# A convolution stage in which ScalarE makes a third tap for half of each piece, and VectorE takes 18 steps instead of 20

## The reference

```python
x = x + _L0_conv_ref(_gn(x), L0_conv_finsler_params)
x = x + _L1_conv_ref(_gn(x), L1_conv_proj_w, ...)
```

```python
out = jnp.einsum('oi,bihw->bohw', proj_w[:, :, 0, 0], x) + proj_b[None, :, None, None]
h = jax.lax.conv_general_dilated(out, dw_w, window_strides=(1, 1), padding=((1, 1), (1, 1)),
                                 feature_group_count=C, dimension_numbers=('NCHW', 'OIHW', 'NCHW'))
h = h + dw_b[None, :, None, None]
```

## Time and profile before

| | |
|---|---|
| median of 3 runs | 10253.23 us |
| the profiled execution: its time, its span | 10254.56 us, 10252.8 us |
| busy share of the span | VectorE 97%, ScalarE 90%, GpSimd 87%, TensorE 84% |
| convolution stage, from the first copy out of PSUM to the last sum | 8700.5 to 9487.6 us |
| resampling stage | 9487.6 us to the end |

### The profile page before, as it was taken

The page is one execution under the profiler, slowest core; times in us unless marked ns, Lnnn a source line. Parts: engine busy times, 40 slices in busy tenths (PEclk is TensorE's granted clock), DMA queues, the critical chain, the costliest instruction groups (busy, mean ns, idle before and its releaser), DMA issues. The chain is left out here.

```text
span 10252.8 us, 72623 instructions
## 1 busy us (share of the span) xinstructions
PE 8565.8 (84%) x18068; PEld 3322.9 (32%) x18068; DVE 9963.9 (97%) x5623; ACT 9179.9 (90%) x6861; POOL 8875.6 (87%) x3274
## 2 busy tenths in 40 slices
PE   2888888888888888888888888888888887998899
PEld 0333333333333333333333333333333333443333
DVE  8999999999999999999999999999999999999999
ACT  2999999999999999999999999999999997888776
POOL 2889888898988999898988888898889887777998
PEclk9999999999999999999999999999999999999999
DMA  8788878888888888888888888888888876444776
GB/s 322 149 157 151 155 155 159 158 160 158 159 157 159 159 158 159 153 159 156 160 155 156 159 158 160 159 158 157 160 159 158 158 141 137 178 182 187 268 282 258
DMA packets 442070, 1751.43 MB, mean 171 GB/s; under 512 B 23888, under 2 KB 130384, under 8 KB 392784
## 3 DMA queue, kind: packets, MB, share of 16 engines
q0 software_dynamic: 278528, 1110.51, 60.9%
q1 hardware_dynamic: 163152, 636.41, 16.6%
HBM read 391.58 MB, written 201.33 MB: 58 GB/s over the span
## 5 line engine op out<-in xcount | busy, mean ns | idle before, releaser
L589 PE MATMUL chain<-dx,mats 128*128 128x512 f32 x10240 | 4979.5, 632 | 940.6 <-ACT chain L639 940.3
L530 POOL TENSOR_TENSOR m<-m,u 128x2048 f32<-128x2048 f32 x1024 | 4338.1, 4350 | 187.1 <-ACT m L621 185.9
L589 PEld LDWEIGHTS chain<-dx,mats 128*128 128x128 f32 x10240 | 1917.0, 197 | 4002.9 <-ACT chain L639 2095.8
L718 DVE SCALAR_TENSOR_TENSOR acc_a<-m,kt,acc_a 128x2048 f32<-128x2048 f32 x1344 | 3162.5, 2353 | 38.2 <-issue 2.4
L639 ACT ACTIVATE chain<-chain,gap_r 128x1024 f32<-128x1024 f32 x2560 | 2694.2, 1086 | 232.2 <-PE chain L589 230.5
L718 DVE SCALAR_TENSOR_TENSOR acc_a<-t,kt,acc_a 128x2048 f32<-128x2048 f32 x1024 | 2411.9, 2355 | 34.2
L501 POOL DMA_DIRECT2D t<-u x1024 | 1486.4, 1563 | 652.8 <-ACT t L621 635.1
L526 POOL TENSOR_TENSOR m<-u,m 128x2048 f32<-128x2048 f32 x384 | 1707.1, 4445 | 0.0
L621 ACT ACTIVATE t<-dx,gap_l 128x2048 f32<-128x2048 f32 x768 | 1540.5, 2006 | 0.4 <-issue 0.4
L589 PE MATMUL chain<-u,mats 128*128 128x512 f32 x3072 | 1456.0, 605 | 71.8 <-ACT chain L639 71.8
L718 DVE SCALAR_TENSOR_TENSOR acc_a<-u,kt,acc_a 128x2048 f32<-128x2048 f32 x576 | 1357.0, 2356 | 20.5
(11 more groups left out here) (149 smaller groups left out, 6876.4 us busy)
## 6 DMA issues: line engine op xcount, KB each, us to landing
t<-u POOLq DMA_DIRECT2D x1024, 1059.0 KB, 8.7
u<-x_dram SPq DMA_DIRECT2D x32, 2688.0 KB, 30.6
xt<-x_dram SPq DMA_DIRECT2D x32, 2048.0 KB, 14.2
x_scratch<-x SPq DMA_DIRECT2D x64, 1024.0 KB, 10.7
h_scratch<-h SPq DMA_DIRECT2D x32, 2048.0 KB, 7.2
both<-h_scratch SPq DMA_DIRECT2D x64, 1024.0 KB, 9.3
out_dram<-res SPq DMA_DIRECT2D x64, 1024.0 KB, 4.9
both<-x_scratch SPq DMA_DIRECT2D x28, 2304.0 KB, 12.6
```

The source lines that it names most:

```text
L530: nc.gpsimd.tensor_tensor(m_tile(j), m_tile(j), rows, ALU.add).then_inc(m_ready, 1)
L589: added = nc.tensor.matmul(chain[h][:, r:r + 2, :], weight, src[:, top:top + 2, dj:dj + W], start=False, stop=True, skip_group_check=True)
L718: nc.vector.scalar_tensor_tensor(out=acc_a[:], in0=src, scalar=k_base, in1=acc_a[:], op0=ALU.subtract, op1=ALU.max).then_inc(a_done, 1)
```

## The change

The second half of each window (its rows 8 to 15; parts q = 2 and 3) gets one tap more from ScalarE: tap 6, which VectorE took before. It goes into the upper half of `tap_b`, once GpSimd has added what lay there, and GpSimd has a fifth add for it. VectorE's chains for q = 2 and 3 have four steps instead of five, 18 in a window. The counts on which the engines wait are changed accordingly. Besides, `tap_a` starts 2 elements (8 bytes) further on in its buffer.

```diff
-        tap_a = [sb(f"tap_a{s}", [P, WR, W]) for s in range(2)]
+        tap_a = [sb(f"tap_a{s}", [P, WR * W + 4])[:, 2:WR * W + 2].rearrange("p (r w) -> p r w", w=W)
+                 for s in range(2)]
...
-        ADDS = 2 * HALVES
-
-        at_step = sorted(((part, k) for part in range(NWIN * PARTS) for k in range(CHAIN)),
-                         key=lambda x: x[0] * CHAIN + 2 * x[1])
+        ACTS = (TAPS_ACT, TAPS_ACT + 1)
+        ALL_ACTS, ADDS = sum(ACTS), sum(ACTS)
+
+        def chain_of(q):
+            return CHAIN + TAPS_ACT - ACTS[q * HALVES // PARTS]
+
+        WSTEPS = sum(chain_of(q) for q in range(PARTS))
+        at_step = sorted(((n * PARTS + q, k) for n in range(NWIN) for q in range(PARTS) for k in range(chain_of(q))),
+                         key=lambda x: x[0] // PARTS * WSTEPS + x[0] % PARTS * CHAIN + 2 * x[1])
...
                 def tap(n, half, which):
                     act.wait_ge(evacuated, n * NPROJ + (4, NPROJ)[half])
+                    lo = half * HALF_ROWS
                     if which == 0:
                         if n >= 2:
-                            act.wait_ge(pool_adds, (n - 2) * ADDS + (2 * half + 2))
+                            act.wait_ge(pool_adds, (n - 2) * ADDS + (2, ADDS)[half])
                             act.wait_ge(h_summed, (n - 2) * 2 + 2)
-                        dst = tap_a[n % 2]
+                        dst = tap_a[n % 2][:, lo:lo + HALF_ROWS, :]
+                    elif which == 1:
+                        if n >= 1:
+                            act.wait_ge(pool_adds, (n - 1) * ADDS + (4, 3)[half])
+                        dst = tap_b[:, lo:lo + HALF_ROWS, :]
                     else:
-                        if n >= 1:
-                            act.wait_ge(pool_adds, (n - 1) * ADDS + (2 * half + 1))
-                        dst = tap_b
-                    t = 9 - TAPS_ACT + which
+                        act.wait_ge(pool_adds, n * ADDS + 1)
+                        dst = tap_b[:, 0:HALF_ROWS, :]
+                    t = 9 - TAPS_ACT + which if which < TAPS_ACT else 9 - TAPS_ACT - 1
...
                     tap(n, 1, 0)
                     tap(n, 1, 1)
+                    tap(n, 1, 2)
...
-                        pool.wait_ge(h_chain, steps_done[n * PARTS + 2 * half + 1, CHAIN - 1])
+                        if half == 1:
+
+                            pool.wait_ge(act_taps, n * ALL_ACTS + ALL_ACTS)
+                            nc.gpsimd.tensor_tensor(tap_a[n % 2][:, rows, :], tap_a[n % 2][:, rows, :],
+                                                    tap_b[:, 0:HALF_ROWS, :], ALU.add).then_inc(pool_adds, 1)
+                            pool.wait_ge(pool_adds, n * ADDS + 4)
+
+                        pool.wait_ge(h_chain, part_done(n * PARTS + 2 * half + 1))
...
-                    if k == CHAIN - 1:
+                    if k == chain_of(q) - 1:
```

More of the change, by code:

```diff
@@ L830, in convolution, with part_done @@
         HALF_ROWS = WR // HALVES
-        ADDS = 2 * HALVES
-        at_step = sorted(((part, k) for part in range(NWIN * PARTS) for k in range(CHAIN)),
-                         key=lambda x: x[0] * CHAIN + 2 * x[1])
+        ACTS = (TAPS_ACT, TAPS_ACT + 1)
[5 more added lines that the diff above has]
+                         key=lambda x: x[0] // PARTS * WSTEPS + x[0] % PARTS * CHAIN + 2 * x[1])
         steps_done = {x: count + 1 for count, x in enumerate(at_step)}
+        def part_done(part):
+            return steps_done[part, chain_of(part % PARTS) - 1]
         def part_of(n, e):
@@ L909, in taps @@
                     if part >= 3:
-                        pe.wait_ge(h_chain, steps_done[part - 3, CHAIN - 1])
+                        pe.wait_ge(h_chain, part_done(part - 3))
                     for r in range(0, QR, 2):
@@ L960, in evacuate @@
                     if e == 0 and n >= 3:
-                        act.wait_ge(h_chain, steps_done[(n - 3) * PARTS + PARTS - 1, CHAIN - 1])
-                        act.wait_ge(act_taps, (n - 2) * (2 * HALVES))
+                        act.wait_ge(h_chain, part_done((n - 3) * PARTS + PARTS - 1))
+                        act.wait_ge(act_taps, (n - 2) * ALL_ACTS)
                     nc.scalar.activation(o[n % 3][:, lo:hi, 1:W + 1], part_of(n, e)[:, at:at + hi - lo, :], ACT.Identity,
@@ L969, in tap @@
                     act.wait_ge(evacuated, n * NPROJ + (4, NPROJ)[half])
+                    lo = half * HALF_ROWS
                     if which == 0:
                         if n >= 2:
-                            act.wait_ge(pool_adds, (n - 2) * ADDS + (2 * half + 2))
+                            act.wait_ge(pool_adds, (n - 2) * ADDS + (2, ADDS)[half])
                             act.wait_ge(h_summed, (n - 2) * 2 + 2)
-                        dst = tap_a[n % 2]
-                    else:
-                        if n >= 1:
-                            act.wait_ge(pool_adds, (n - 1) * ADDS + (2 * half + 1))
-                        dst = tap_b
-                    t = 9 - TAPS_ACT + which
+                        dst = tap_a[n % 2][:, lo:lo + HALF_ROWS, :]
[3 more added lines that the diff above has]
+                        dst = tap_b[:, lo:lo + HALF_ROWS, :]
+                    else:
+                        act.wait_ge(pool_adds, n * ADDS + 1)
+                        dst = tap_b[:, 0:HALF_ROWS, :]
+                    t = 9 - TAPS_ACT + which if which < TAPS_ACT else 9 - TAPS_ACT - 1
                     ty, tx = divmod(t, 3)
-                    lo = half * HALF_ROWS
-                    nc.scalar.activation(dst[:, lo:lo + HALF_ROWS, :],
+                    nc.scalar.activation(dst,
                                          o[n % 3][:, lo + ty:lo + ty + HALF_ROWS, tx:tx + W], ACT.Identity,
@@ L1012, in _ @@
                     for which in range(2):
-                        sum_h(NWIN - 1, which, slice(half * HALF_ROWS, (half + 1) * HALF_ROWS), to, 2 * half + 2)
+                        sum_h(NWIN - 1, which, slice(half * HALF_ROWS, (half + 1) * HALF_ROWS), to, (2, ADDS)[half])
             @block.gpsimd
@@ L1020, in _ @@
                         rows = slice(half * HALF_ROWS, (half + 1) * HALF_ROWS)
-                        pool.wait_ge(act_taps, n * (2 * HALVES) + 2 * half + 2)
+                        pool.wait_ge(act_taps, n * ALL_ACTS + 2 * half + 2)
                         nc.gpsimd.tensor_tensor(tap_a[n % 2][:, rows, :], tap_a[n % 2][:, rows, :], tap_b[:, rows, :],
```

## The result

| | before | changed |
|---|---|---|
| median | 10251.93 us (4 runs) | 10336.31 us (4 runs) |
| profiled execution: time, span | 10254.56, 10252.8 us | 10335.66, 10333.5 us |

The ratio of the changed kernel to the one before is 1.0082, with a 95% interval of 1.0067 to 1.0097: 84 us slower. The forecast was slower by 45 us, 10298.4 us, in a range up to 10312. The side was right, the size not: nearly half of the loss had not been seen.

What follows compares the result with a forecast made beforehand. ScalarE's list with its wait was to replace VectorE as the bound, 25.30 us a window against 23.82. First windows 4.0, 28 windows x 1.48 = 41.4, tail -0.2: 45.2 us on 10253.2 gives 10298.4 us, range 10287 to 10312.

Steps and rivals of the forecast that it cites:

- What bounds the kernel: Convolution stage: VectorE's 20 steps set the 23.82 us window, with ScalarE nearly as full.
- The third tap, 1.98 us on ScalarE, and 0.42 us of cover: Before piece 4, ScalarE's added tap takes 1.98 us and covers 0.42 us of idle time there.
- So from the small copies to that of piece 2 it takes 8.30 us, whatever VectorE does: ScalarE's stretch between these copies stays 8.30 us, including 2.50 us of wait for TensorE's piece 2.
- TensorE waits there, not ScalarE: Between pieces 3 and 4, ScalarE takes 7.06 us against TensorE's 5.59, so TensorE does the waiting.
- VectorE's idle time at `h`: Before writing part 0 into `h`, VectorE idles some 3.8 us a window for ScalarE's second sum, at no cost.
- GpSimd: Five adds a window, 19.1 us at 3.82 each or 22.8 at 4.56, stay under the 25.3 us window.
- The line of the earlier trace: Support for the shift: a dilation add with its tile put 2 off modulo 4 takes 3.81 us.
- The tail: After window 31's piece 4: -0.2 us in the total, or 6 us longer with adds at 4.56 us.
- VectorE keeps setting the pace: Rival: VectorE stays the bound and the window shrinks to 21.4 us; -75 us, 10178 us; chance 0.05.
- the 2.50 us go: Rival: ScalarE bounds without its wait before piece 2; 22.8 us window, -31 us, 10222 us; chance 0.03.

Runs made afterwards that it cites:

- e5: The kernel before with VectorE's lower-half chains cut to four steps, tap 6 left out there and nothing in its place; 10241.2 us, ratio 0.9987.
- e1: The changed kernel with six extra TensorE matmuls of 256 columns a window, whose result nothing reads, ahead of piece 1; 10297.7 us, ratio 1.0043.
- e3: The changed kernel with ScalarE's first upper tap between the copies of pieces 1 and 2, first lower tap ahead of piece 3's copy; 10241.9 us, ratio 0.9990.
- e10: The kernel before with ScalarE's taps ahead of the copies of pieces 2 and 3, TensorE's taps of q = 2 ahead of piece 1; 10256.3 us.
- e6: The changed kernel with `tap_a` back at its old offset; 10345.4 us, ratio 1.0089.

## Why the prediction was wrong, point by point

- **What bounds the kernel: right.** VectorE set the pace by 0.43 us a window, and ScalarE's list with its wait for piece 2 stood right behind it. e5 measured that distance.
- **The third tap, 1.98 us on ScalarE, and 0.42 us of cover: right.** Three taps took 5.96 us in the changed kernel. Five windows are 25.29 us long, and with the clock up (e1) all are; forecast 25.30.
- **"So from the small copies to that of piece 2 it takes 8.30 us, whatever VectorE does": this is the step that failed.** It holds in five windows and is 10.00 us in 23. The term was mis-sized: I took TensorE's 7.1 us of it (piece 1, taps of q = 2, piece 2) from a trace in which TensorE comes to it after 0.88 us of idle time, and carried it into a kernel in which, by my own sum, TensorE waits more. The prediction even says so ("TensorE waits there, not ScalarE") and costs it at nothing. That sentence means the place ahead of piece 4; in the trace all 3.56 us lie ahead of piece 1. Idle time of TensorE was not free: behind it the clock falls, and piece 1 heads the one run of TensorE for which ScalarE waits. With the clock down, piece 1 and the taps of q = 2 take 6.92 us from start to start (8922.86 to 8929.78) instead of 5.23. The price is 1.70 us, 23 times: 39 of the 84 us.
- **The trace of before had it, once.** In window 3, behind a stall of ScalarE, TensorE was idle for 3.41 us, and the window was 24.86 us long while the three after it took 23.39 to 23.40, at the pace without VectorE. TensorE's timeline and the stretch, of the kernel before:

```profile
8789.54 3.44 PE L901 MATMUL pp<-both,wg 128*128 128x512 f32 x4 [3.41 <-ACT o L964]
```

```profile
8789.50:8793.10 3.60, 3.56 (x5) 1.70 (x6) 2.68 (x3) 3.60 (x3) 3.55 (x1) 0.58 0.00 0
```

- **VectorE's idle time at `h`: right.** 3.8 us forecast, 3.62 measured; TensorE waited for VectorE 5.2 us in the whole stage, once, in window 31. VectorE's wait for TensorE, 49.3 us, was not in the prediction; in e1 it is 1.0 us before the steps into PSUM in windows 3 to 30, where the changed kernel has 37.7, so it came with the slow clock.
- **GpSimd: right.** Adds of 3.82 us, and no window from 3 on is longer with 4.55. The line of the earlier trace rows was weak support: it is one of 1024 adds of L530 whose median is 4.27 us, while the 64 of `dv` all lie at 3.82. The tail is 36.8 us (9530.93 to 9567.7), as worked out; without the shift it is 6 us longer, as worked out. Not foreseen was the later load, which makes window 2 longer by 1.9 us without the shift.
- **The rivals:** that VectorE keeps setting the pace is ruled out by e5 even with nothing added. That the 2.50 us go was given too little thought as something to do: with one PSUM buffer TensorE can't be earlier, but ScalarE can do something else meanwhile (e3). A fall of the clock was no rival at all, and should have been the first one on the slower side.

Still open: how the falls are decided. Gaps of 2.26 to 3.56 us gave the same 23 of 28 windows, with a beat of five or six windows between those that were spared, and the fall comes some 0.3 us later in each window of such a row. In e3 one gap of 3.47 us in window 3 passed without a fall, while falls followed a gap of 1.92 us in e10 and the two short gaps of e6. So the length of the gap alone does not decide it. The runs fix what the clock costs here and that filling the gap to 0.97 us ends it, not where the limit is.

## What to carry to other kernels

When a change makes one engine's list the longer one, the others' idle time grows; for TensorE, ask where this idle time gathers, and whether what follows it is waited for. If it is, price it with the clock down, from any place in the trace where a matmul group comes slow behind a gap. And before work is moved onto an engine that is nearly full, look for the wait in its list: moving an instruction of its own into that wait took the changed kernel from 27.0 to 23.4 us a window here, 1.7 of it from the clock that no longer falls and 1.9 from the wait itself. Two steps taken off the engine that bounded the kernel before gave 0.4 (23.8 to 23.4).

## What the runs showed of the hardware

- A matmul group of 4 x 512 columns took 1.96 us at granted clock 1.00 and 3.54 at 0.54, behind 3.56 us of idle time; a gap of 2.26 us had the same effect, in 23 of 28 windows.
- In the 23 slow windows of the changed kernel the granted clock was still 1.00 through 3.56 us of idle time and fell on the work behind it, in one of them over 1.1 us after TensorE had started again.
- Extra matmuls that nothing reads made the kernel 39 us faster (10336.3 to 10297.7).
- GpSimd's add of two inputs of 2048 elements takes 4.55 us where both start at the same offset, and 3.82 where one lies 8 bytes off.
